# A four-layer Flamingo-style block on one core: three reduced-precision passes for the first attention's output projection, another order at the end of the last layer, and re-laid buffers

## The reference, cut to what matters

```python
x = x + tanh(g_xattn[0]) * xattn0(layernorm(x), ctx)   # 16 heads of 32, context of 128 tokens, biases   -> stage A
x = x + tanh(g_ffn[0])   * ffn0(layernorm(x))          # top 256 of 2048 tokens: attention and a gated MLP -> stage C
x = x + tanh(g_xattn[1]) * xattn1(layernorm(x), ctx)   # 16 heads of 64                                   -> stage D
x = x + tanh(g_ffn[1])   * ffn1(layernorm(x))          # quantised 512 -> 2048, 3-tap conv, silu, quantised -> stage E
# xattn0: q = x Wq + bq ; k, v from ctx ; p = softmax(q k / sqrt(32)) ; o = p v ; return o Wo + bo
```

## Time and profile before

| | us |
|---|---|
| median of 3 executions (lowest, highest) | 1777.56 (1774.46, 1781.29) |
| the profiled execution's own time | 1780.38 |
| its span | 1778.7 |
| PE matmul busy | 1555.4 (87%) |
| DVE busy | 1276.5 (72%) |
| ACT busy | 885.8 (50%) |
| POOL busy | 574.2 (32%) |

### The profile page before, as it was taken

How to read it: one execution, slowest core, us unless ns; L and a number is a source line. 1 busy time by engine, 2 the same in 40 slices (tenths; PEclk the granted TensorE clock), 3 DMA queues, 4 the chain that set the end, 5 groups by cost and what they waited for, 6 DMA issues and landing times. The chain is left out here.

```text
span 1778.7 us, 25649 instructions
## 1 busy us (share of the span) xinstructions
PE 1555.4 (87%) x9526; PEld 951.3 (53%) x9559; DVE 1276.5 (72%) x2070; ACT 885.8 (50%) x1427; POOL 574.2 (32%) x556
## 2 busy tenths in 40 slices
PE   6798888998769979878999999999997778888887
PEld 5444444443346648655666665666664434544443
DVE  5576678878543546654677776777766599999996
ACT  3455555554445426425334333433433477777774
POOL 3133334223310002123122021112200297777781
PEclk9899999998879889989999999999999899999998
DMA  4112211222633524631021101102011330211211
GB/s 162 48 48 95 96 64 56 72 72 87 229 110 109 185 87 142 201 113 48 1 70 39 60 25 60 60 24 83 1 60 36 120 125 14 78 70 67 73 63 48
DMA packets 73283, 142.34 MB, mean 80 GB/s; under 512 B 8417, under 2 KB 17781, under 8 KB 72906
## 3 DMA queue, kind: packets, MB, share of 16 engines
q1 hardware_dynamic: 71914, 137.55, 22.5%
q0 software_dynamic: 960, 3.15, 0.6%
q10 hardware_dynamic: 288, 0.00, 0.0%
HBM read 97.67 MB, written 43.01 MB: 79 GB/s over the span
## 5 line engine op out<-in xcount | busy, mean ns | idle before, releaser
L2916 POOL TENSOR_TENSOR E_y<-E_y,E_centre 128x1024 f32<-128x1024 f32 x64 | 151.1, 2361 | 6.6 <-ACT E_y L2945 3.5
L1458 ACT ACTIVATE D_oT<-D_OB 128x512 fp32r<-128x512 f32 x64 | 38.3, 598 | 220.1 <-DVE D_OB L1775 220.1
L2804 PE MATMUL E_HP<-E_xT,E_w1q 128*128 128x512 bf16 x482 | 124.3, 399 | 2.5 <-DMA E_w1q<-w1b_d 0.8
L2908 POOL TENSOR_SCALAR E_centre<-E_hs,E_cw,E_cb 128x512 f32<-128x512 f32 x64 | 109.2, 1707 | 52.6 <-DVE E_hs L3004 52.5
L1747 DVE TENSOR_TENSOR D_q_low<-D_PJ,D_q_high 128x512 fp32r<-128x512 f32 x60 | 41.5, 691 | 97.5 <-ACT D_q_high L1434 97.5
L2829 PE MATMUL E_YT<-ident,E_y 128*128 128x128 f32 x496 | 67.8, 282 | 42.8 <-DVE E_am L3022 39.0
L3013 DVE SCALAR_TENSOR_TENSOR E_y<-E_hs,E_cw,E_y 128x512 f32<-128x512 f32 x128 | 104.8, 857 | 0.0
L2817 PE MATMUL E_OP<-E_w2q,E_yb 128*128 128x512 bf16 x446 | 103.1, 385 | 0.7 <-issue 0.7
L1527 PE MATMUL D_PJ<-D_xT_high,D_wq_high 128*128 128x512 f32 x240 | 101.7, 424 | 0.2
L591 PE MATMUL A_TX<-A_wo,A_oT 128*128 128x512 f32 x176 | 90.0, 636 | 7.1 <-PEq L1109 7.1
L1527 PE MATMUL D_PJ<-D_xT_high,D_wq_low 128*128 128x512 f32 x240 | 95.0, 396 | 0.0
(11 more groups left out here) (436 smaller groups left out, 4131.8 us busy)
## 6 DMA issues: line engine op xcount, KB each, us to landing
A_res<-in_x SPq DMA_DIRECT2D x8, 1024.0 KB, 5.7
xn_d<-A_xn SPq DMA_DIRECT2D x8, 1024.0 KB, 4.6
x_d<-A_res SPq DMA_DIRECT2D x8, 1024.0 KB, 5.4
W_raw<-in_w1T SPq DMA_DIRECT2D x16, 512.0 KB, 3.5
W_raw<-in_w2T SPq DMA_DIRECT2D x16, 512.0 KB, 3.8
D_res<-x_d SPq DMA_DIRECT2D x8, 1024.0 KB, 5.9
x_d<-D_res SPq DMA_DIRECT2D x8, 1024.0 KB, 4.4
E_res<-x_d SPq DMA_DIRECT2D x8, 1024.0 KB, 5.5
```

Of the source, the lines that this page charges most:

```text
L2804: mm = pe.matmul(HP[:, i % 2, e, :], w1q[:, k, m * P:(m + 1) * P], XT[n % 2][:, k, :], start=k == 0, stop=k == KD - 1)
L2908: pool.tensor_scalar(U[i % 2][:, 0, :], hs[i % NBUF][:, 0, 1:TILE + 1], cw[:, 2 * p, 1:2], cb[:, 2 * p:2 * p + 1], ALU.mult, ALU.add).then ...
L2916: pool.tensor_tensor(y, y, U[i % 2][:, :, :], ALU.add).then_inc(t0, 1)
```

## The change

Three things are changed together.

1. Stage A's output projection. `A_wo` is split once into a high and a low half (`scale_wo` on ACT makes the high one right after the scaling, `low_wo` on POOL the low one), and so is each slot's `A_oT`: `divide` now writes back into the bank A_OB, ACT copies the high half out (`high_o`), and DVE subtracts it for the low half (`low_o`). `project_out` then makes three fp32r passes a k where one f32 pass stood. `score` moves ahead of `add_out` on DVE, `low_o` stands behind it. `weigh` of the next slot waits for `low_o`.
2. Stage E's end. On PE `project_out` of lap 6 chunk 1 moves ahead of `turn_y(60)`, and chunk 2 ahead of `turn_y(62)`. On DVE `add_out` of chunk 0 moves ahead of `quantise` of chunk 2, and of chunk 1 ahead of `right_taps(62)`.
3. Buffers laid over each other: raw weights and halves share room, the chosen rows lie over the halves of x, so `gather` waits for the last query projection; two scratch tiles become bf16.

```diff
 def gather(pool, b):
     pool.wait_ge(id_ok, 2 * (b + 1))
+    pool.wait_ge(q_mm, QT * STEPS)
...
 def project_out(pe, n, c, part, parts):
     if part == 0:
         pe.wait_ge(o_ok, QT * (n + 1))
+    h, l = oh[n % 2], ol[n % 2]
     for k in range(part * QT // parts, (part + 1) * QT // parts):
-        mm = pe.matmul(out_bank(n, c), oT[n % 2][:, k, c * P:(c + 1) * P], wo[:, k, :],
-                       start=k == 0, stop=k == QT - 1)
+        for o, w in ((h, woh), (h, wol), (l, woh)):
+            mm = pe.matmul(out_bank(n, c), o[:, k, c * P:(c + 1) * P], w[:, k, :],
+                           start=k == 0 and o is h and w is woh, stop=k == QT - 1 and o is l)
...
+def low_wo(k):
+    pool.wait_ge(wo_hi, k + 1)
+    pool.tensor_tensor(wol[:, k, :], wo[:, k, :], woh[:, k, :].bitcast(F32), ALU.subtract).then_inc(wo_ok, 1)
...
 def scale_wo(k):
...
-    act.activation(wo[:, k, :], wo[:, k, :], ACT.Copy, scale=tg).then_inc(wo_ok, 1)
+    act.activation(wo[:, k, :], wo[:, k, :], ACT.Copy, scale=tg).then_inc(wo_sc, 1)
+    act.wait_ge(wo_sc, k + 1)
+    act.activation(woh[:, k, :], wo[:, k, :], ACT.Copy).then_inc(wo_hi, 1)
+
+def high_o(s):
+    act.wait_ge(o_div, s + 1)
+    act.activation(oh[s // GROUPS % 2][:, s % GROUPS, :], OB[:, :], ACT.Copy).then_inc(o_hi, 1)
...
     keep_row(act, s)
     keep_sums(act, s)
+    high_o(s)
     keep_found(act, s)
     if turn_x:
         keep_xT(n + 2, 2)
...
 def weigh(s):
     n, j = divmod(s, GROUPS)
+    need(pe, o_ok, s)
...
 def divide(s):
     dve.wait_ge(pv, s + 1)
-    dve.tensor_tensor(oT[s // GROUPS % 2][:, s % GROUPS, :], OB[:, :], rz[:, :], ALU.mult).then_inc(o_ok, 1)
+    dve.tensor_tensor(OB[:, :], OB[:, :], rz[:, :], ALU.mult).then_inc(o_div, 1)
+
+def low_o(s):
+    dve.wait_ge(o_hi, s + 1)
+    dve.tensor_tensor(ol[s // GROUPS % 2][:, s % GROUPS, :], OB[:, :],
+                      oh[s // GROUPS % 2][:, s % GROUPS, :].bitcast(F32), ALU.subtract).then_inc(o_ok, 1)
...
     divide(s)
+    score(dve, s)
     add_out(dve, s)
-    score(dve, s)
+    low_o(s)
...
 turn_y(END - 5)
+project_out(LAST - 1, 1)
 turn_y(END - 4)
-project_out(LAST - 1, 1)
 turn_y(END - 3)
+project_out(LAST - 1, 2)
 turn_y(END - 2)
 turn_y(END - 1)
-project_out(LAST - 1, 2)
 spread(LAST)
...
+            if n == LAST and p == ADD[0]:
+                add_out(n - 1, 0)
             if p in QUANT:
                 quantise(n - 1, QUANT.index(p))
...
+add_out(LAST - 1, 1)
 right_taps(END - 2)
 biggest(END - 4)
 right_taps(END - 1)
-add_out(LAST - 1, 1)
```

More of the change, by code:

```diff
@@ L161, in context_tensors @@
     sb = lambda n, s, d: ctx.enter_context(nc.sbuf_tensor(L["name"] + n, s, d))
-    kh, kl = (sb(n, [P, L["inner"] // P, NB, CTX], F32R) for n in ("k_high", "k_low"))
-    return kh, kl, sb("V", [P, NB, L["inner"]], F32)
+    shape = [P, L["inner"] // P, NB, CTX]
+    kh = sb("k_high", shape, F32R)
+    with ExitStack() as over:
+        kT = over.enter_context(nc.sbuf_tensor(L["name"] + "kT", shape, F32))
+    return kh, sb("k_low", shape, F32R), sb("V", [P, NB, L["inner"]], F32), kT
 class ContextStage:
@@ L345, in chosen_tensors @@
     sb = lambda n, s, d=F32: ctx.enter_context(nc.sbuf_tensor("S_" + n, s, d, side="right"))
-    return {"idx": sb("idx", [P, NB * HALVES], mybir.dt.uint32), "xs": sb("xs", [P, NB * HALVES, D]),
-            "base": sb("base", [P, NB * HALVES, D]), "got": ctx.enter_context(nc.semaphore("S_gathered"))}
+    with ExitStack() as over:
+        halves = [over.enter_context(nc.sbuf_tensor(f"A_xT_{n}", [P, KD, TILE], F32R, side="right")) for n in ("high", "low")]
+    return {"xs": sb("xs", [P, NB * HALVES, D]), "base": sb("base", [P, NB * HALVES, D]),
+            "idx": sb("idx", [P, NB * HALVES], mybir.dt.uint32), "xT_halves": halves,
+            "got": ctx.enter_context(nc.semaphore("S_gathered"))}
 def by_act(q):
@@ L384, in narrow_attention @@
         upto, less, ties = keep("upto", [P, NC]), keep("less", [P, CHUNKS]), keep("ties", [P, CHUNKS])
-        later, lost = keep("later", [P, NB, NC, NC]), keep("lost", [P, NC])
+        later, lost = keep("later", [P, NB, NC, NC], BF16), keep("lost", [P, NC])
         rank = keep("rank", [P, NC])
@@ L392, in narrow_attention @@
         X = sb("x", [P, SUB, D])
-        xt = [sb(f"xT{i}", [P, KD, P]) for i in range(2)]
-        xh, xl = sb("xT_high", [P, KD, TILE], F32R), sb("xT_low", [P, KD, TILE], F32R)
+        with ExitStack() as over:
+            xt = [over.enter_context(nc.sbuf_tensor(f"{name}xT{i}", [P, KD, P], F32, side="right")) for i in range(2)]
+        above = keep("above", [P, S], BF16)
+        xh, xl = chosen["xT_halves"]
         qh, ql = sb("q_high", [P, QT, TILE], F32R), sb("q_low", [P, QT, TILE], F32R)
-        oT = [sb("oT0", [P, QT, TILE]), oT_last]
-        wq = oT_last[:, :, :].rearrange("p q n -> p (q n)").rearrange("p (k n) -> p k n", k=KD)
+        oT = [sb("oT0", [P, 2, QT, TILE], F32R), oT_last]
+        oh, ol = [o[:, 0, :, :] for o in oT], [o[:, 1, :, :] for o in oT]
         pr = sb("probs", [P, HG, TILE])
@@ L773, in _ @@
                 for c in range(SUB):
+                    if n == 0 and c:
+                        low_wo(c - 1)
                     if c == 1 and ahead:
@@ L788, in _ @@
                                 .then_inc(biased, 1)
+                    if n == 0 and c == SUB - 1:
+                        low_wo(c)
                     if n == STEPS - 1 and c == 1:
```

37 lines of the change are left out of this document (22 added, 15 removed).

## The result

Over 20 executions of each kernel the medians are 1774.68 us with the change and 1780.83 without it, 6.2 us apart. The measured ratio is 0.996 with a 95% interval of 0.9947 to 0.9972, that is faster by about 7.1 us (5.0 to 9.4). The forecast was 1765 us, a gain of 13.2. The direction was right. The size was about twice too large, and the gain does not come from where the forecast had put it.

A forecast was written before the change was run, and what follows sets the result against it. It took stage A's slots to be held by PE and DVE in turn, with waits at stage E's end. Stage A's 10.0 plus stage E's 3.2 made 13.2 us off the profiled 1780.38; against the median it said 1765, range 1757 to 1776.

The forecast's parts named there:

- Half of `project_out`, 0.42 us less: Stage A on PE: six fp32r matmuls take 1.54 us where half a projection took 1.98, call it 0.42 less.
- From slot 0 to slot 1 +0.7: Stage A's first block: gain per lap 0.7 us, only 0.3 in laps 4 and 6, -0.2 in lap 5; 2.5 in all.
- From slot 2 over slot 3 to the next query projection, +4.4: Stage A: gains 1.1 us in laps 1, 2, 5, where PE holds slot 3; 0.4 in 3 and 4; 0.3 in 6.
- A DVE round grows by 0.15, say 0.2 us: Stage A slots held by DVE: `low_o` adds 0.69 us, the earlier `score` offsets most; five `ln_stats` rounds lose 1.0 in all.
- Laps 1 to 6, +5.9: Stage A's first block: summed gain of 5.9 us from the slot terms 2.5, -1.0 and 4.4.
- slower: the clock: Rival, stage A: PE idles more, query projections fall to 1.2 GHz, 2.6 us lost each; 1788 us, chance 0.08.
- Lap 7, +3.2: Stage A's last lap, no query projection: both projection halves count, 0.8 us in each of four slots.
- Lap 0, -0.9: Stage A, slot 3: `high_o` delays the third copy of x, for which `transpose_x` 3 waits; 0.9 us lost once.
- Second block, +1.8: Stage A's second block: four whole projections 3.4 us shorter in all, of which 1.8 counts, between 1.4 and 2.2.
- Stage E, +3.2: Stage E's end: moved projections and adds gain 2.5, 0.3 and 0.4 us; at worst 1.5 is left.
- the two terms ahead of it, +0.3 and +0.4: Stage E: chunk 1's `add_out` moved ahead of `right_taps(62)` gives 0.3 us; `turn_y(63)` after shorter PE idle gives 0.4.
- ACT and DVE give the gain back: Rival, stage A: `low_o` waits for a late `high_o` in 14 rounds, 8.4 us lost; 1773 us, chance 0.30.

## Why the prediction was wrong in size

Two steps failed. In stage A, the sum took PE's shorter projection as the gain and what changes on DVE as a correction of 0.15 us a round; in laps 1 to 6 the gain is the score's place, and DVE's subtraction takes most of it back. In stage E, the sum held that the 2.5 us of DVE's wait "stay"; projections at half clock take most of them. Term by term:

**Half of `project_out`, 0.42 us less.** Too large. "From its first start to its last end" set a modelled end of the f32 matmuls (1.98) against a count of starts. From start to the next instruction's start it is 1.89 before and 1.58 after: 0.31. In the second block, where whole projections stand free, one goes from 3.52 us to 2.83 (A_PJ, 471.75 - 468.23 and 464.77 - 461.94): 0.69 where 0.84 was taken.

**From slot 0 to slot 1 +0.7, with both halves counted.** Where DVE had room ahead of its maxima, from slot 1's start to slot 2's, it is +0.3 in each of laps 1 to 6 (10.57 to 11.07 us before, 10.25 to 10.77 after), the second half alone. The first half's gain ended at once against DVE's maxima. With lap 5, where a loss had been forecast, this makes 1.9 us in all against 2.5, so it is not the large miss.

**From slot 2 over slot 3 to the next query projection, +4.4.** This is the large miss. Over laps 1 to 5, for which the sum had 4.1 us less, the stretch grew by 3.9 (159.7 us over four profiles before, 163.6 over five after). In lap 1, where neither kernel has half clock in it, it goes from 29.7 to 30.2 us, where 1.1 less was forecast: PE was said to hold slot 3, but it now waits for DVE's maxima in nearly every slot. With the score moved alone the same stretch takes 29.0, without the low half 28.4, so `low_o` costs 1.8 us there, more than twice its own 0.69. The stretch from slot 0's query projection to slot 1 became 3.3 us shorter over laps 1 to 6, in part because less half clock falls into slot 0 (23.9 us against 27.3 in the first pair of profiles).

**A DVE round grows by 0.15, say 0.2 us.** Right where it was measured (0.25 in slot 14), and its parts stand separately: `low_o` is the 8.7 us of the run without the low half, and the score's place the 9 us of the run with the score alone. I had added them up as if they were a small correction to PE's gain; they are the two large terms, and PE's shorter work is the small one in laps 1 to 6 (1.6 us, or 5.6 if the run with the low half on POOL is set against the score alone). It pays outside these laps.

**Laps 1 to 6, +5.9.** Over the profiles +2.0. Besides the points above, the part of the clock is missing. The rival "slower: the clock" was right in kind and too large as a case: the trace's stretches at half clock sum to 41.0 us in laps 1 to 6 in four of five changed profiles and to 30.7 in three of four before, and the windows read 0.94 and 0.95. That is up to 5 us, an estimate for a PE that is busy all through the 10.3 us more. The clock fell in slots of the kind of slot 14, where the prediction's sentence against it ("the new idle is at most 0.6 us longer") was true of the idle (2.52 against 1.93; in slots 6 and 10 it grew by 0.9 and 0.7) and wrong as a reason.

**The Trainium skill** (TensorE: Matmul & The Clock Gate, Part 1), by which the gate closes after idleness, was weighed as a rule against shortening PE's work where DVE sets the pace. The runs agree: laps 1 to 6 have a granted clock of 0.96 with the score moved and the full f32 work, 0.94 with three passes, 0.92 with two. The run with the low half on POOL has 0.95 with three passes, so the clock does not follow from PE's work alone.

**Lap 7, +3.2.** Over the profiles +1.8; both kernels have two lengths there (47.9 and 51.2; 46.6 and, once, 52.2), and like against like it is 1.3 (47.9 against 46.6).

**Lap 0, -0.9.** Measured -2.0. The wait for the copy grew from 1.00 to 1.88, that is by the 0.9 of the forecast. The other 1.1 lies in lap 0 ahead of it, where single profiles differ as much (before 44.3 to 47.3, changed 46.0 to 48.5), and no run shows the change to be its cause.

**Second block, +1.8.** Measured +4.1. The block's first projection, its last turned row and the next stage's context projections, before and after:

```profile
462.98 5.07 PE L591 MATMUL A_TX<-A_wo,A_oT 128*128 128x512 f32 x8 [7.11 <-PEq L1109]
...
483.05 0.48 PE L602 MATMUL A_SC<-ident,A_own_scores 128*128 128x128 f32 x1 [1.39 <-DVE A_own_scores L654]
483.32 2.77 PE L211 MATMUL A_SC<-D_ctxT,D_wk 128*128 128x256 f32 x6
```

```profile
456.73 0.77 PE L606 MATMUL A_TX<-A_wo_high,A_oT 128*128 128x512 f32 x1 [6.66 <-PEq L1147]
...
475.79 0.32 PE L617 MATMUL A_SC<-ident,A_own_scores 128*128 128x128 f32 x1 [1.09 <-DVE A_own_scores L669]
475.95 1.47 PE L210 MATMUL A_SC<-D_ctxT,D_wk 128*128 128x256 f32 x6
```

Up to the last turned row it is 1.0 (20.07 against 19.06). Behind it, work that the change leaves alone went from the low clock to the high one (2.77 against 1.47 for the same six matmuls): in this block the clock gave back some of what it took in the laps. That more came than the 1.8 is luck of this kind: 57.2 to 57.8 us in the four profiles before and 53.3 to 53.5 in the five after, so it repeats, but nothing in the forecast had asked for it.

**Stage E, +3.2.** From the sixth last maximum to the last `add_out` it is 42.7 us over five profiles with the old order (41.8 to 43.5) and 41.9 over eleven with the new one (40.9 to 42.2): 0.8. By time alone it is 3.6, with an interval of 1.1 to 6.1, which takes in the forecast and leaves out 0.8; two more pairs with and without the new end differ by 1.6 us (0.9984 and 0.9975, the changed stage A) and 0.2 us (0.9973 and 0.9972, the score moved), so time alone leaves the size open, and the 0.8 is what the profiles show.

The step that failed is "so the gain stays": the 2.5 us do go from DVE's wait, but the chunk 3 projection behind an idle of 2.22 us pays 1.7 of them at half clock. Over the profiles 0.6 is left behind the reciprocal, and the two terms ahead of it, +0.3 and +0.4, came to 0.3 (22.1 to 21.9 us from the sixth last maximum to the reciprocal, 20.6 to 20.0 from there to the end).

Ahead of the reciprocal two things met. The moved `add_out` runs while POOL adds (1738.59 to 1740.96) and takes 0.74 us, no more than at its old place, and the pair behind it takes 1.64 us instead of 2.27. But the chunk 2 projection too now runs mostly at half clock, 5.14 us where it took 4.43 before and would take 3.45 at the full one, and DVE waits for the turn behind it. The prediction named half clock as its worst case, for chunk 3 alone, at 1.5 left, and should have taken it for the likely one. It read 3.61 us as chunk 1's, but that row is chunk 3's; chunk 1, like chunk 2 in the earlier trace rows, took 4.5 us behind an idle PE:

```profile
1740.12 4.53 PE L2817 MATMUL E_OP<-E_w2q,E_yb 128*128 128x512 bf16 x15 [0.22 <-issue]
```

Without the +0.3 its sum is 2.9 and not the 2.8 that it gives.

**Sum.** 2.0 + 1.8 - 2.0 + 4.1 = 5.9 in stage A against 10.0, and 0.8 in stage E against 3.2: 6.7, near the measured 7.1. A part of that is luck, since the laps came 3.9 us under the forecast and the second block 2.3 over it, and since stages C to E are left out: the whole spans of the same nine profiles differ by 3.2 us. The rival "ACT and DVE give the gain back" had the right size (4.8) by the wrong wait. DVE hardly waited for ACT's high half (waits of 40 to 460 us: total, times, longest):

```profile
DVE A_oT L1109 <- ACT A_oT L869: 2.7, 4, 0.7
```

What stays open is whether stages C to E, which the change does not touch, are 2 to 3 us longer with it, as the means of the profiles have it; the timed executions, with 7.1 us (5.0 to 9.4), leave room for under 2 us of it beside a sum of 6.7.
